# Expert stages: the first choice's half of the 0/1 matrix made by ScalarE in two activations, instead of by a GpSimd comparison

## What is computed

```python
logits = jnp.einsum('btc,ce->bte', x, router_w) + router_b
cap = int(LOAD_FACTOR * K * Tt // E)                      # 76 places of each of 8 experts in a batch
top_k_logits, expert_indices = jax.lax.top_k(logits, K)   # K = 2 choices of every row
pos = jnp.cumsum(one_hot, axis=0) * one_hot - 1           # the row's place in its expert's queue
expert_inputs = buf.at[ei.ravel(), pos.ravel()].add(xr)   # rows past the 76th are dropped
h = jnp.einsum('eti,eih->eth', einp2, w_c_fc) + b_c_fc
g = jnp.einsum('eti,eih->eth', einp2, w_gate) + b_gate
o = jnp.einsum('eth,eho->eto', jax.nn.silu(h * g), w_c_proj) + b_c_proj
out = jnp.sum(pr[..., None] * o[i, p], axis=1)            # two rows gathered back, weighted
```

## Time and profile before

| | |
|---|---|
| time, median of 3 runs | 2454.76 us |
| the profiled execution: its own time, its span | 2458.44 us, 2456.4 us |
| mean granted TensorE clock, share of full | 0.973 |
| VectorE (DVE) busy | 1603.0 us, 65% |
| ScalarE (ACT) busy | 1289.9 us, 53%, 2670 instructions |
| GpSimd (POOL) busy | 774.3 us, 32%, 896 instructions |
| first expert stage / second expert stage | from about 505 to 1060 us / from about 1880 us to the end |

### The profile page before, as it was taken

One profiled execution on the slowest core, in us unless ns is written; L12 is line 12 of the kernel. 1 busy time (PEld: TensorE's weight loads), 2 busy tenths in 40 slices (PEclk: granted clock), 3 DMA queues, 4 the chain that ended last, 5 costly groups with the idle time before them and its releaser, 6 DMA issues.

```text
span 2456.4 us, 46634 instructions
## 1 busy us (share of the span) xinstructions
PE 2290.1 (93%) x14634; PEld 1823.5 (74%) x14634; DVE 1603.0 (65%) x5069; ACT 1289.9 (53%) x2670; POOL 774.3 (32%) x896
## 2 busy tenths in 40 slices
PE   5989998988999999889999999999998989999994
PEld 4978887977777777667777777777776876776774
DVE  8867776867667775446655656565656666767653
ACT  3755545744444444356566666666653444444441
POOL 6602220036546775320000000000001455766644
PEclk9999999999999999899999999999999999999997
DMA  7040000000111111100000000000000001111222
GB/s 256 0 163 0 0 0 1 0 6 23 28 28 41 41 39 44 41 20 0 0 0 0 0 0 0 0 0 0 0 0 1 18 23 34 46 48 48 51 57 53
DMA packets 71019, 68.04 MB, mean 28 GB/s; under 512 B 9712, under 2 KB 58352, under 8 KB 70512
## 3 DMA queue, kind: packets, MB, share of 16 engines
q1 hardware_dynamic: 61360, 47.62, 6.2%
q0 software_dynamic: 8192, 16.79, 3.1%
q10 hardware_dynamic: 1344, 2.16, 0.3%
HBM read 32.47 MB, written 34.08 MB: 27 GB/s over the span
## 4 chain that ended last, share of the span: by engine, by line
PE 46%; DVE 3%; issue 3%; ACT 1%; POOL 1%; another core or an unknown queue 1%; DMA 0%; ACTq 0%; DVEq 0%; POOLq 0%; SPq 0%
PE moe_bank L1745 5%; PE lin_bank L1117 5%; PE lin_bank L1043 5%; PE lin_bank L1051 5%; PE lin_bank L1070 4%; PE lin_bank L1062 4%; PE moe_bank L1731 4%; PE moe_bank L1735 4%; PE lin_bank L1093 4%; PE lin_bank L1109 2%; PE moe_bank L1719 2%; PE lin_bank L1080 1%; POOL all_landed L1564 1%; DVE moe_hot L1910 1%
## 5 line engine op out<-in xcount | busy, mean ns | idle before, releaser
L1809 ACT ACTIVATE moe_fc<-moe_bank,all_b_fc 128x380 f32<-128x380 f32 (+2 forms) x512 | 262.0, 513 | 338.9 <-PE moe_bank L1731 291.4
L1920 DVE SCALAR_TENSOR_TENSOR moe_act<-moe_bank,all_b_moe_gate,moe_fc 128x380 f32<-128x380 f32 (+2 forms) x512 | 270.4, 531 | 203.7 <-PE moe_bank L1735 114.5
L1731 PE MATMUL moe_bank<-moe_rowsT,all_w_fc 128*128 128x380 f32 (+2 forms) x1024 | 359.7, 434 | 17.6 <-ACT moe_fc L1809 11.1
L1735 PE MATMUL moe_bank<-moe_rowsT,all_w_gate 128*128 128x380 f32 (+2 forms) x1024 | 353.8, 428 | 13.3 <-DVE moe_act L1920 9.2
L1745 PEld LDWEIGHTS moe_bank<-all_w_proj,moe_act 128*128 128x128 f32 x2688 | 324.8, 197 | 12.4 <-ACT moe_act L1816 1.8
L1745 PE MATMUL moe_bank<-all_w_proj,moe_act 128*128 128x128 f32 x2688 | 332.6, 281 | 1.4 <-ACT moe_act L1816 1.4
L1564 POOL DMA_INDIRECT all_landed<-rows_out,all_take_at x256 | 274.0, 1070 | 157.5 <-issue 121.6
L1735 PEld LDWEIGHTS moe_bank<-moe_rowsT,all_w_gate 128*128 128x128 f32 x1024 | 189.8, 194 | 102.5 <-DVE moe_act L1920 12.7
L1280 POOL COPY lin_xn_ones<-lin_xn 128x254 f32<-128x254 f32 x32 | 12.8, 401 | 744.9 <-PE lin_bank L1051 744.5
L1642 POOL TENSOR_SCALAR moe_hot<-all_slot_ids,moe_slot 128x608 bf16<-128x608 f32 x120 | 219.0, 1829 | 87.9 <-issue 53.1
L1816 ACT ACTIVATE moe_act<-moe_act 128x760 f32<-128x760 f32 (+2 forms) x256 | 181.4, 708 | 104.3 <-DVE moe_act L1920 91.4
(11 more groups left out here) (190 smaller groups left out, 4374.5 us busy)
## 6 DMA issues: line engine op xcount, KB each, us to landing
rows_out<-moe_expert_out SPq DMA_DIRECT2D x80, 128.0 KB
rows_out<-all_zeros SPq DMA_DIRECT2D x1, 9728.0 KB, 28.3
rows_out<-moe_expert_out SPq DMA_DIRECT2D x80, 62.0 KB
all_landed<-rows_out,all_take_at POOLq DMA_INDIRECT x256
out<-all_x SPq DMA_DIRECT2D x5, 640.0 KB
rows_out<-moe_expert_out SPq DMA_DIRECT2D x48, 64.0 KB
all_w_fc<-in_w_fc SPq DMA_DIRECT2D x1, 2048.0 KB, 10.0
all_w_gate<-in_w_gate SPq DMA_DIRECT2D x1, 2048.0 KB, 14.0
```

The costliest lines, as they stand in the source:

```text
L1731: nc.tensor.matmul(bank[FC + j % 2][:, 0:c.width], k.w_fc[:, e, j * P:(j + 1) * P], rowsT[:, c.n % 2, e, 0:c.width], start=True, stop=True ...
L1735: nc.tensor.matmul(bank[GATE + j % 2][:, 0:c.width], k.w_gate[:, e, j * P:(j + 1) * P], rowsT[:, c.n % 2, e, 0:c.width], start=True, stop= ...
L1809: nc.scalar.activation(fc[:, j, 0:c.width], bank[FC + j % 2][:, 0:c.width], ACT.Identity, bias=k.b_fc[:, e * MC + j:e * MC + j + 1]).then_ ...
L1920: nc.vector.scalar_tensor_tensor(act_in[:, i % 2, j, 0:c.width], bank[GATE + j % 2][:, 0:c.width], k.b_moe_gate[:, e * MC + j:e * MC + j + ...
```

## The change

The comparison leaves GpSimd. ScalarE makes the same ones in two activations a tile: `distance = |place - slot|` for all 608 places, stored as bf16, then `relu(1 - distance)`, which is one where the distance is zero and zero elsewhere. It does so in two slots of its own, lags 6 and 7, one tile in each, as the last thing ScalarE does in the slot. The second activation waits for the first.

```diff
-ROUTE_LAGS = {"norm": 0, "transpose": 1, "router": 2, "mask": 3, "count": 4, "assign": 5, "hot0": 8, "hot1": 9,
+ROUTE_LAGS = {"norm": 0, "transpose": 1, "router": 2, "mask": 3, "count": 4, "assign": 5, "first0": 6, "first1": 7, "hot0": 8, "hot1": 9,
               "send0": 10, "send1": 11}
...
+        distance_sb = k.sem("distance_ready")
+        distance = k.sb("distance", [P, EXPERTS * CAP], BF16)
...
-                def first_choice(b):
-                    pool.wait_ge(routed, b + 1)
-                    pool.wait_ge(sent_ps, 2 * (b - 2) + 2)
-                    for t in range(TILES):
-                        nc.gpsimd.tensor_scalar(hot[:, b % 2, t, :], k.slot_ids[:, :], slot[:, b % 2, t, 0:1], None,
-                                                ALU.is_equal).then_inc(hot_first, 1)
...
-                        if "assign" in work:
-                            first_choice(work["assign"])
...
+                def first_choice(b, t):
+
+                    n = TILES * (b - OWN) + t
+                    act.wait_ge(routed, b + 1)
+                    if t == 0:
+                        act.wait_ge(sent_ps, 2 * (b - 2) + 2)
+                    if n:
+                        act.wait_ge(hot_first, n)
+                    nc.scalar.activation(distance[:, :], k.slot_ids[:, :], ACT.Abs, bias=slot[:, b % 2, t, 0:1],
+                                         scale=-1.0).then_inc(distance_sb, 1)
+                    act.wait_ge(distance_sb, n + 1)
+                    nc.scalar.activation(hot[:, b % 2, t, :], distance[:, :], ACT.Relu, bias=1.0, scale=-1.0).then_inc(hot_first, 1)
...
+                        for t in range(TILES):
+                            if f"first{t}" in work:
+                                first_choice(work[f"first{t}"], t)
```

## The result

| | before | changed |
|---|---|---|
| time, median of 4 runs each, same chip | 2455.48 us | 2548.46 us (2544.81 to 2552.48) |
| ratio | | 1.0379, 95% interval 1.0364 to 1.0395 |
| the profiled execution: its own time, its span | 2458.44, 2456.4 us | 2552.48, 2550.4 us |
| mean granted TensorE clock | 0.973 | 0.963 |
| VectorE / ScalarE / GpSimd busy | 1603.0 / 1289.9 / 774.3 us | 1596.4 / 1444.3 / 538.9 us |

The change costs 93 us. The forecast was 43, and the result lies outside its range. The direction was right, half of the size was missing.

A forecast was written before the change was run, and what follows sets the result against it. TensorE's work was taken to set the pace, with second choices on the path without slack. Delays of 21.2 and 21.9 us in the two stages, +43.1, took 2458.44 to 2501.5, by the runs' median 2498 us; range 2470 to 2520.

The forecast's parts named there:

- What goes: GpSimd's 120 comparisons, 219 us, nearly all beside other work; their going gains 4.1 us at a late gather in chunk 1.
- the second rival: The rival "It costs more": a pair of 1.67 us and a lower TensorE clock in narrow chunks, 2524 us; chance 0.14.
- The pair: ScalarE's two activations for one tile, distance then relu: 1.5 us together, 180 us of ScalarE over both stages.
- The wide chunks: 380-column chunks 2 to 5: 2.35 us each, from +0.85 in the first batch, +0.2 second, +1.3 fifth.
- third and fourth: 0: Third and fourth batches of a 380-column chunk: no delay, as VectorE and TensorE are late enough for other reasons.
- some 30: TensorE's idle time until second choices, over the kernel: to rise from 7.6 us to some 30.
- The narrow chunks: Chunks 0 and 1, shorter slots with the same pair: 6.8 us for chunk 0; 4.0 and 4.7 for chunk 1.
- The landing waits of chunk 1: VectorE's combine waits 2.41 and 1.69 us for a gather behind a comparison; both go, a gain of 4.1 us.
- The relief: VectorE's combines and second choices without GpSimd's comparisons: 5.2 us by the medians, little on the path; taken as nothing.
- The rule: GpSimd and VectorE contend for SBUF in two-input operations; as fourth rival, faster by less contention, 2445 us, chance 0.02.
- The wide chunks did not absorb it: First rival: VectorE's small gaps take up the wide chunks' delays, only narrow chunks pay 24.3 us, 2479; chance 0.15.
- It costs more: Second rival: a pair of 1.67 us (+14 us) and TensorE's clock in four narrow chunks (+12), 2524 us; chance 0.14.

The follow-up runs named there:

- s1_paced: The changed kernel with GpSimd waiting for `routed` again at the slot of assign, comparing nothing; 2514.03 us on chip 6, ratio 1.0254.
- s3_after_spread: The changed kernel with groups of four gathers held until VectorE's multiply of their slot (six slots earlier in chunk 7); 2501.13 us on chip 6, ratio 1.0205.
- x4_nobody: The changed kernel with the first choice left out, made by no engine; 2403.01 us on chip 7, ratio 0.9932.
- x2_both: The changed kernel with GpSimd also comparing, into a tile nobody reads, and the distance kept in `hot`; 2478.90 us on chip 7, ratio 1.0252.
- x1_half: The changed kernel with tile 0's first choice back on GpSimd, only tile 1's on ScalarE; 2421.87 us on chip 7, ratio 1.0008.
- x3_apart: The changed kernel with each relu one slot after its distance, three slots per batch, distance kept in `hot`; 2429.49 us on chip 7, ratio 1.0040.
- y1_skip: The changed kernel with the second tile's pair in slot 8 instead of 7, plus GpSimd's wait for `routed`; 2435.45 us on chip 9, ratio 1.0068.

## Why the prediction was wrong, and where it was right

**The step that failed** stands under "What goes". It took the comparison for work and priced its going by what waits for its result and by one late gather. But the comparison was also a wait. `pool.wait_ge(routed, b + 1)` stood on GpSimd's queue between two groups of gathers, and went with it. I moved the later work forward only where that gave something, in chunk 1, and never asked in what rhythm the queue would run without it. The price is what the change cost on the first chip beyond what it cost without stops (changed on chip 9, before on chip 1). By chunks of the second stage: 3.7, 4.4 and 4.7 us in chunks 3 to 5 and 10.8 in chunk 6 (11.7 on the first chip against 0.9), less 3.6 in chunk 1; 20.5 us with the rest, and 22.3 in the first stage. By the medians of the runs it is 93.0 - 52.6 = 40.4 us. Of the 3.8% s1_paced gives back 1.3 points, and the holds of s3_after_spread another 0.5. That runs of gathers stop the others was to be read in the trace of before already: the run of 16 in its chunk 7, with stops of up to 7.5 us.

**The clock, which the sum put at nothing.** Only the second rival had a term for TensorE's clock, 12 us. These are the two chunks 0 (first `bias_fc` to the next chunk's) of the kernel before, then of the changed one, both on the first chip, with columns as in the earlier trace rows:

```profile
522.15:566.58 44.43, 38.66 (x308) 35.01 (x307) 27.29 (x108) 23.04 (x63) 18.34 (x18) 1.00 0.04 12
1898.02:1943.62 45.60, 40.20 (x308) 36.62 (x307) 27.18 (x108) 23.11 (x62) 18.34 (x18) 0.96 0.04 12
```
```profile
521.10:576.31 55.21, 46.02 (x308) 39.60 (x307) 26.66 (x108) 30.69 (x74) 7.38 (x12) 0.88 0.04 9
1945.76:1999.32 53.56, 43.92 (x308) 37.99 (x307) 26.57 (x108) 30.59 (x75) 7.37 (x12) 0.94 0.04 10
```

The same 308 products keep TensorE busy for 7.4 and 3.7 us longer, at a lower granted clock. In the first one of the changed kernel it stood at 0.5, the level of 1.2 GHz, from 534.1 to 540.9 and from 551.2 to 558.0; TensorE had waited 1.67 us for `moe_fc` until 533.5, and 1.04 us until 549.6. So 11.1 of the 18.7 us that the two chunks lost are a slower TensorE, and 7.7 are waits. Without stops it is much the same: against 38.7 us in each chunk 0 of the kernel before on chip 1, the changed kernel keeps TensorE busy 44.0 and 43.4 us there and 46.0 and 43.3 on chip 9. Over the whole program TensorE's busy time rose by 25 us on the first chip, for as many products, and by 10 to 16 on the chips without stops.

**The pair**: 0.79, 0.71, together 1.5 us as put. Right.

**The wide chunks**: 2.35 us forecast, 2.9 to 3.0 measured in chunks 3 to 5 without the stops and 4.1 in chunk 2. The first batch's delay came as 0.63 for 0.85 and the fifth's as 0.64 for 1.3; the "third and fourth: 0" was wrong, there is a wait of 1.06 between them. Two of the three are waits for the mask, which I had not followed: the delayed multiplication pushes VectorE's mask chain for the next batch as well as the second choice. In the first chip's numbers TensorE's waits for masks grew by 19 us and those for second choices by 18, where I had put them all on the second choices (7.6 to "some 30": 25.4).

**The narrow chunks**: for chunk 0, 6.8 us were forecast; measured were 10.8 and 8.0 in the two stages of the first chip, 10.9 and 7.9 on chip 9, 9.5 and 8.5 on chip 1; over both stages more than half of that is the clock. The waits alone, 7.7 us for both, are less than the 13.6 of the sum. For chunk 1, 4.0 and 4.7 were forecast, and 2.1 and 4.2 measured on chip 9, 2.1 and 0.6 on the first chip. Chunk 6 came as 0.9 for 1.0. The landing waits of chunk 1 went as put.

**The relief**: "I take nothing" beside the 4.1 us of landings. x4_nobody shows 17 with them, x2_both 6 to 8 in the changed kernel. I had read medians over minima, 16 ns a combine; the mean was 43 ns above what it is without comparisons. The Trainium skill (GPSIMD Engine Reference, Key points) has the two engines contend for SBUF in VectorE's operations with two SBUF inputs. The combines, which are such operations, agree: 392, 370 and 350 ns in the mean with 120, 60 and no comparisons. The rule spoke against my sign and was right; what it gave was outweighed by the pairs.

**The rivals.** The wide chunks did not absorb it. "It costs more" had the right direction, 2524, from a dearer pair and a lower clock. The pair was not dearer. The clock's part was there: its 12 us are about what the two chunks 0 show, 10 to 12 us of longer busy time. It was a cause that the forecast left out, but not the one that made 93 us out of some 53. Without the stops the sum is near: +43.1 forecast, +51 to +53 measured on chips 1 and 9, a ratio of 1.0176 for 1.0217, inside the range. Part of that is luck: waits of chunk 0 put too high, and a relief, seen mainly in chunk 1, put at nothing, stand against a clock left out and wide chunks put too low. The forecast's list of what a removed instruction does was short.

**Why two pairs cost 50 us and one costs 2.** Both are net of the relief. The runs say that neither the sum of ScalarE's work nor the full slot decides, but two full slots in a row (x1_half, x3_apart, y1_skip). Part of the step is the clock: TensorE is busy 2271 us in x1_half, 2275 in x3_apart, 2279 in y1_skip and 2284 to 2289 in the changed kernel, for the same products. A reading of the rest that fits, not shown by itself: TensorE runs ahead of ScalarE by two banks of `moe_fc`. One slot in which ScalarE is late is taken up there and won back in the next; the second in a row finds the lead used.

## What to carry to other kernels

An instruction that leaves a queue takes its waits with it: write down the queue's rhythm without them, and look in the old trace for a place that already has that rhythm. Work that goes onto an engine with room on average wants a free slot between two loads: the same 3 us per batch cost, net, 53 us in two neighbouring slots, 18 with a slot between them and 9 spread over three. Where new waits of TensorE appear, give the clock a term of its own in the sum: here it took more of the two chunks 0 than the waits did. Read the cost of contention from the mean, not from the median.

## What the runs showed of the hardware

Long runs of gathers on GpSimd (one each 1.3 us) held up what waits for TensorE by up to 9.2 us, on chips 5 and 6 and on the first one, whose number is not known (the kernel before at 2452 to 2455 us). On chips 1, 7, 9 and 15 (2417 to 2420) runs of up to 20 gathers held up nothing. Where the stops came, groups of four cost nothing or a stop of 0.9 to 1.4 us, runs of 8 some 4 us a chunk, a run of 12 between 1 and 6 (chunk 6 before, and in s1_paced), one of 16 from 12 to 18 (chunk 6 changed, chunk 7). Whether TensorE itself is late there, with records whose ends are modelled, or only its signals are, the profile doesn't tell; that waits for VectorE were answered within 0.1 us in the same time, it does, in the window shown. Nor is it known what the chips differ in; it was not tried. A single chip's result for this change, 2.2% or 3.8%, was exact to 0.2% on each and wrong for the other.

A GpSimd comparison made the combines that it overlapped slower, 454 ns in the mean for 347.

The best version on a chip with stops was the kernel before with its gathers held (0.31% faster), on one without them VectorE's first choice (0.14% faster, under what counts). The two were not run together.
